# Key blocks of a cross-attention kernel: one PSUM read by ScalarE, and the low halves made from SBUF by GpSimd and VectorE

## The reference

```
x = layernorm(x + self_attention(x))
kv = ctx @ wkv.T + bkv;  k, v = split(kv)          # ctx: (16, 1500, 256)
q = qdq(x) @ qdq(wq).T + bq                        # int8-like rounding
p = softmax(q k^T / sqrt(16));  o = p v            # 16 heads
x = layernorm(x + qdq(o) @ qdq(wp).T + bp)
x = layernorm(x + experts(x))                      # top 2 of 8
```

## Time and profile before

| | |
|---|---|
| median of 3 runs | 853.0 us (848.32 to 858.43) |
| the profiled execution | 854.35 us, its span 852.5 us |
| mean granted TensorE clock | 0.986 |
| PE busy | 774.4 us, 91% of the span |
| DVE busy | 638.2 us, 75% |
| ACT busy | 511.5 us, 60% |
| POOL busy | 296.9 us, 35% |
| the chain that ended last | PE 57%, DVE 13%, DMA 11%, ACT 10%, issue 6% |

### The profile page before, as it was taken

How to read it: one execution, slowest core, us unless ns; L and a number is a source line. 1 busy time by engine, 2 the same in 40 slices (tenths; PEclk the granted TensorE clock), 3 DMA queues, 4 the chain that set the end, 5 groups by cost and what they waited for, 6 DMA issues and landing times.

```text
span 852.5 us, 30042 instructions
## 1 busy us (share of the span) xinstructions
PE 774.4 (91%) x12379; PEld 582.8 (68%) x12379; DVE 638.2 (75%) x1234; ACT 511.5 (60%) x1084; POOL 296.9 (35%) x366
## 2 busy tenths in 40 slices
PE   5689989999998999999999999999898899999996
PEld 3366666576666666666666666666665579999995
DVE  5877777868877878785977778786875745688887
ACT  2347656566565657655665666666665543787772
POOL 3263216223712371254126421732270003143232
PEclk9899999999999999999999999999999899999999
DMA  7356554554645546554655655565467976766643
GB/s 228 91 167 174 169 155 139 156 160 128 179 129 159 164 143 180 164 143 138 178 156 141 173 169 147 154 171 156 121 186 208 307 258 161 225 190 209 210 136 98
DMA packets 91380, 143.27 MB, mean 168 GB/s; under 512 B 11423, under 2 KB 79583, under 8 KB 87918
## 3 DMA queue, kind: packets, MB, share of 16 engines
q1 hardware_dynamic: 87742, 136.74, 53.6%
q0 software_dynamic: 3504, 4.62, 2.8%
HBM read 101.60 MB, written 39.68 MB: 166 GB/s over the span
## 4 chain that ended last, share of the span: by engine, by line
PE 57%; DVE 13%; DMA 11%; ACT 10%; issue 6%; SPq 1%; POOL 1%; DVEq 0%; POOLq 0%; ACTq 0%
PE ps L1659 15%; PE ps L1652 11%; DMA sums<-y_sb,g_token 10%; PE ps L1733 7%; PE ps L1711 6%; DVE negmax L522 4%; ACT pT L1441 3%; ACT k_front L1414 3%; PE ps L1971 3%; PE ps L1675 3%; DVE k_front L516 2%; PE ps L1992 2%; PE ps L1776 2%; PE ps L1620 2%; PE ps L1743 2%
## 5 line engine op out<-in xcount | busy, mean ns | idle before, releaser
L522 DVE TENSOR_REDUCE negmax<-ps 112x1 f32<-112x1500 f32 x121 | 207.4, 1714 | 32.1 <-PE ps L1675 31.9
L1441 ACT ACTIVATE pT<-ps 125x448 f32<-125x448 f32 x384 | 195.7, 546 | 21.9 <-PE ps L1711 18.2
L1265 POOL TENSOR_TENSOR ctx_lo<-ctx_raw,ctx_hi 128x250 f16<-128x250 f32 x188 | 119.3, 666 | 182.4 <-DVE ctx_hi L507 182.4
L1711 PE MATMUL ps<-qbd,k_st 97*128 97x112 f16 x1536 | 127.8, 214 | 17.3 <-ACT pT L1441 8.7
L1711 PEld LDWEIGHTS ps<-qbd,k_st 97*128 97x128 f16 x1536 | 91.2, 98 | 73.6 <-ACT pT L1441 20.1
L1397 ACT COPY v_sb<-ps 125x512 f32<-125x512 f32 x96 | 56.4, 587 | 83.5 <-PE ps L1659 83.4
L516 DVE SCALAR_TENSOR_TENSOR k_front<-ps,bk_sb,k_front 128x500 f16<-128x500 f32 x80 | 58.8, 735 | 63.0 <-ACT k_front L1414 63.0
L1733 PE MATMUL ps<-pT,v_sb 125*17 125x56 f32 x6144 | 92.1, 215 | 12.2 <-issue 12.2
L1733 PEld LDWEIGHTS ps<-pT,v_sb 125*17 125x17 f32 x6144 | 79.9, 98 | 31.9 <-issue 20.1
L1414 ACT ACTIVATE k_front<-ps,bk_sb 128x500 f16<-128x500 f32 x80 | 54.3, 678 | 62.3 <-PE ps L1652 62.3
L1659 PE MATMUL ps<-wkv_hi,ctx_hi 128*125 128x256 f16 x384 | 76.6, 281 | 10.5 <-DVE k_front L516 9.0
(11 more groups left out here) (263 smaller groups left out, 1492.7 us busy)
## 6 DMA issues: line engine op xcount, KB each, us to landing
k_st<-k_dram SPq DMA_DIRECT2D x288, 125.0 KB, 3.0
w_sb<-w SPq DMA_DIRECT2D x25, 1024.0 KB, 5.2
ctx_raw<-ctx_T SPq DMA_DIRECT2D x48, 500.0 KB, 3.7
k_dram<-k_front SPq DMA_DIRECT2D x80, 250.0 KB, 3.0
xs<-zeros SPq DMA_DIRECT2D x28, 260.0 KB, 4.4
w_sb<-w SPq DMA_DIRECT2D x8, 512.0 KB, 5.2
k_dram<-k_back SPq DMA_DIRECT2D x16, 250.0 KB, 2.9
xg<-xs SPq DMA_DIRECT2D x21, 130.0 KB, 4.1
```

The lines of the kernel that those rows point to most:

```text
L522: V.tensor_reduce(negmax[0:QW], ps[0:QW, BANK_S:BANK_S + CHUNKS, 0:MC], AX.XY, ALU.max, negate=True).then_inc(max_done, 1)
L1265: last = nc.gpsimd.tensor_tensor(ctx_lo[:, k, c2, a], ctx_raw[:, k, c2, a], ctx_hi[:, k, c2, a], ALU.subtract)
L1441: nc.scalar.activation(pT[0:MT, (PAIRS * b + p) % 3, TPC * g:TPC * g + TPC], ps[0:MT, BANK_T + n % 2, 0:TPC * QW].rearrange("p (t n) -> p ...
L1711: last = mm(ps[:, BANK_T + n % 2, QW * i:QW * i + QW], k_st[:, j, p, a:a + P], qbd[:, j, p].rearrange("p h s -> p (h s)"), start=True, sto ...
```

## The change

ACT now reads a key block from PSUM once and writes it as f32 to SBUF (`k_full`, a ring of three); this releases the bank (`unit_out`). DVE rounds that copy to the f16 high half (`tensor_copy` into the ring `k_two`, also of three), after a wait for the store of the block three before it. The remainder is a subtraction of two SBUF operands: on GpSimd as two pieces of 250 columns (`k_lo_step`), and on DVE as one piece of 500 columns (`key_low`) for all six blocks of batch 0 and, in slot 3 of each even batch, for units 0 and 2 of the odd batch being prepared. The stores wait for the remainder (`k_lo_done`). `two_batches` is as before.

```
         def unit_step(b, par, u):
             if g in KEYS:
-                i = key_place(c, g)
-                dve.wait_ge(unit_done, UNITS * b + u + 1)
-                dve.wait_ge(k_hi_done, len(KEY_UNITS) * b + KEY_UNITS.index(u) + 1)
-                V.scalar_tensor_tensor(k_two[i][:, 1], ps[:, BANK_KV, 0:MC], bk_sb[:, g:g + 1], k_two[i][:, 0],
-                                       ALU.add, ALU.subtract).then_inc(unit_out, 1)
+                n = key_number(b, u)
+                dve.wait_ge(unit_out, UNITS * b + u + 1)
+                if n >= 3:
+                    dve.wait_ge(*stored(n - 3))
+                V.tensor_copy(k_two[:, n % 3, 0], k_full[n % 3]).then_inc(k_hi_done, 1)
+                if b == 0:
+                    key_low(b, u)
+        def key_low(b, u):
+            n = key_number(b, u)
+            dve.wait_ge(k_hi_done, n + 1)
+            dve.wait_ge(k_lo_done, n)
+            V.tensor_tensor(k_two[:, n % 3, 1], k_full[n % 3], k_two[:, n % 3, 0], ALU.subtract).then_inc(k_lo_done, 1)
...
                     if units_on:
                         for u in unit_slots(slot):
                             unit_step(b + 1, 1 - j, u)
+                    if slot == 3 and j == 0:
+                        key_low(b + 1, 0)
+                        key_low(b + 1, 2)
...
             def store_keys(b, u, between=()):
-                sp.wait_ge(unit_out, UNITS * b + u + 1)
+                sp.wait_ge(k_lo_done, n + 1)
                 if not (isinstance(b, int) and b == 0):
                     sp.wait_ge(k_in[g], loaded(b - 1))
-                sp.dma_start(k_dram[i], k_two[i]).then_inc(stored(b, u)[0], 16)
+                sp.dma_start(k_dram[i], k_two[:, n % 3]).then_inc(stored(n)[0], 16)
...
+            def k_lo_step(b, u):
+                n = key_number(b, u)
+                pool.wait_ge(k_hi_done, n + 1)
+                if b % 2 == 1 and u == 5:
+                    pool.wait_ge(k_lo_done, n)
+                for half in range(2):
+                    a = slice(MC // 2 * half, MC // 2 * half + MC // 2)
+                    last = nc.gpsimd.tensor_tensor(k_two[:, n % 3, 1, a], k_full[n % 3][:, a], k_two[:, n % 3, 0, a], ALU.subtract)
+                last.then_inc(k_lo_done, 1)
             def iteration(it, t_before):
-                ctx_lo_step(2 * it + 1, 1, 1)
+                b = 2 * it + 1
+                ctx_lo_step(b, 1, 1)
...
                 kbd_step(it + 1)
-                ctx_lo_step(2 * it + 1, 1, 2)
-                ctx_lo_step(2 * it + 2, 0, 0)
+                ctx_lo_step(b, 1, 2)
+                k_lo_step(b, 5)
+                k_lo_step(b, 6)
+                k_lo_step(b, 8)
+                ctx_lo_step(b + 1, 0, 0)
                 if t_before is not None:
                     b_rstd_step(t_before)
-                ctx_lo_step(2 * it + 2, 0, 1)
+                k_lo_step(b, 11)
+                ctx_lo_step(b + 1, 0, 1)
+                k_lo_step(b + 1, 0)
+                k_lo_step(b + 1, 2)
                 rstd_step(it + 1)
-                ctx_lo_step(2 * it + 2, 0, 2)
+                ctx_lo_step(b + 1, 0, 2)
+                k_lo_step(b + 1, 5)
+                k_lo_step(b + 1, 6)
+                k_lo_step(b + 1, 8)
                 qbd_step(it + 1, 0, 0)
-                ctx_lo_step(2 * it + 3, 1, 0)
+                ctx_lo_step(b + 2, 1, 0)
                 qbd_step(it + 1, 0, 1)
+                k_lo_step(b + 1, 11)
...
             def k_hi_step(b, u):
                 c, g = UNIT[u]
-                i = key_place(c, g)
-                if b > 0:
-                    act.wait_ge(*stored(b - 1, u))
+                n = key_number(b, u)
                 act.wait_ge(unit_done, UNITS * b + u + 1)
-                nc.scalar.activation(k_two[i][:, 0], ps[:, BANK_KV, 0:MC], ACT.Identity,
-                                     bias=bk_sb[:, g:g + 1]).then_inc(k_hi_done, 1)
+                if n >= 3:
+                    act.wait_ge(k_lo_done, n - 2)
+                nc.scalar.activation(k_full[n % 3], ps[:, BANK_KV, 0:MC], ACT.Identity, bias=bk_sb[:, g:g + 1]).then_inc(unit_out, 1)
```

More of the change, by code:

```diff
@@ L161, in decoder_layer @@
         wkv_lo = sb("wkv_lo", [P, CH, 2 * D], F16)
-        k_front = sb("k_front", [P, 5, 2, MC], F16)
+        k_two = sb("k_two", [P, 3, 2, MC], F16)
+        k_full01 = sb("k_full01", [P, 2, MC])
         sb("behind_k_front", [P, 8], F32)
@@ L168, in decoder_layer @@
         k_st = sb("k_st", [KA, 2, PAIRS, M + 4], F16)
-        k_back = sb("k_back", [P, 2, MC], F16)
+        k_full2 = sb("k_full2", [P, MC])
         sb("behind_keys", [P, 616])
@@ L220, in decoder_layer @@
         b_oqT = a_t2[:, D:D + P].bitcast(BF16).rearrange("p (c n) -> p c n", c=CH)
-        k_two = [k_front[:, n] for n in range(5)] + [k_back]
+        k_full = [k_full01[:, 0], k_full01[:, 1], k_full2]
         staging = pT[:].rearrange("p a m n -> p (a m n)")
@@ L273, in decoder_layer @@
         k_hi_done = sem("k_hi_done")
+        k_lo_done = sem("k_lo_done")
         unit_out = sem("unit_out")
@@ L434, in key_place, with key_number, stored @@
             return CH * c + g
-        def stored(b, u):
-            n = KEY_UNITS.index(u)
-            return k_out[n % 2], 16 * (len(KEY_UNITS) // 2 * b + n // 2 + 1)
+        def key_number(b, u):
+            return len(KEY_UNITS) * b + KEY_UNITS.index(u)
+        def stored(n):
+            return k_out[n % 2], 16 * (n // 2 + 1)
         def loaded(b):
@@ L1082, in store_keys @@
                 c, g = UNIT[u]
-                i = key_place(c, g)
-                sp.wait_ge(unit_out, UNITS * b + u + 1)
+                i, n = key_place(c, g), key_number(b, u)
+                sp.wait_ge(k_lo_done, n + 1)
                 if not (isinstance(b, int) and b == 0):
                     sp.wait_ge(k_in[g], loaded(b - 1))
-                sp.dma_start(k_dram[i], k_two[i]).then_inc(stored(b, u)[0], 16)
+                sp.dma_start(k_dram[i], k_two[:, n % 3]).then_inc(stored(n)[0], 16)
                 for dst, src in between:
@@ L1094, in load_keys @@
                 i = key_place(c, g)
-                sp.wait_ge(*stored(b, u))
+                sp.wait_ge(*stored(key_number(b, u)))
                 for r, part in enumerate(KEY_PARTS[c]):
@@ L1293, in qbd_step @@
                     pool.wait_ge(st_done, CHUNKS * PAIRS * (2 * t + j - 1))
-                if j == 1:
+                if j == 1 and (h == 1 or t == 0):
                     pool.wait_ge(qbd_done, 8 * t + 4 + 2 * h)
+                elif j == 1:
+                    pool.wait_ge(k_lo_done, 2 * len(KEY_UNITS) * t + len(KEY_UNITS))
+                elif h == 0 and not first:
+                    pool.wait_ge(k_lo_done, 2 * len(KEY_UNITS) * t + len(KEY_UNITS) - 1)
                 elif first and h == 0:
@@ L1375, in _ @@
             ctx_lo_step(B - 1, 1, 2)
+            k_lo_step(B - 1, 5)
             b_rstd_step(TILES - 2)
+            for u in (6, 8, 11):
+                k_lo_step(B - 1, u)
             scatter(TILES - 2)
```

## The result

| | before | after |
|---|---|---|
| median of the runs | 853.3 us (4 runs) | 906.3 us (4 runs, 903.3 to 910.3) |
| ratio, 95% interval | | 1.062 (1.055 to 1.070) |
| profiled execution, its span | 854.35, 852.5 us | 903.31, 901.5 us |
| mean granted TensorE clock | 0.986 | 0.953 |

The change makes the kernel 53 us slower. The forecast was 885, slower, with a range from 860 to 908. The sign and the main mechanism were right, the size was short by 21 us.

A forecast was written before the change was run, and what follows sets the result against it. PE was taken to set the pace nearly everywhere. Terms -11 (release, shorter piece), +2 (door), +1 (start), +33 (even batches), +2 (odd), +5 (clock) gave +32: 885 us beside the 853.0 median, range 860 to 908.

The forecast's parts named there:

- The release and the shorter piece: PE's waits on the PSUM bank, 8 us won, and DVE's cast at 0.42 us, 3 us won: 11 us, bounds 3 and 17.
- the door's +2: DVE's 96 casts held by POOL: 16 us of DVE's queue, about one eighth on the chain, 2 us, bounds 0 and 12.
- The two engines at one door: DVE's casts and subtractions from SBUF can be held for one POOL piece; a cast waits 0.17 us on average.
- The stalls in even batches: Slot 4's scores wait for unit 11's loads behind the store moved to slot 3: 33 us in eight batches, bounds 25 and 44.
- its door term: Within the even batches' stall, slot 3's first subtraction held by POOL's `kbd` pieces: 0.3 us, bounds 0 and 1.04.
- The odd batches: Unit 0's remainder on POOL delays the same store and loads; cover 1.6 us in seven batches, 2 us added, bounds 0 and 10.
- The clock: TensorE falls to 1.2 GHz behind 4 of eight stalls: 5 us more, bounds 0 and 14.
- small terms: 1 us at the start, from batch 0's six remainders on DVE, and 2 us for the odd batches.
- A: Rival: unit 11's load isn't late, so only the release counts, 844 us; chance 0.06.
- B: Rival: no change, with shorter stalls of 25 us, the gain at its bound of 17 and the clock holding, 861; chance 0.08.
- C: Rival: DVE becomes the bound, each of 96 casts held for a full POOL piece, odd batches at their bound, 912; chance 0.08.

The follow-up runs named there:

- the kernel with the early subtractions: The changed kernel, with VectorE making the remainders of units 0 and 2 of odd batches right behind their casts in slots 1 and 2: 845.6 us, repeated 845.1 us.
- all remainders on GpSimd: The changed kernel, with GpSimd also making the remainders of units 0 and 2 of odd batches, in slot 2 ahead of `kbd`: 861.9 us, 1.010.
- the late store alone: The kernel before, with the store of unit 0 of each odd batch waiting for `nm_row` of slot 3 of the batch ahead: 905.7 us, 1.059.
- `kbd` behind: The changed kernel, with GpSimd's `kbd_step` waiting until VectorE has made the remainders of units 0 and 2: 895.6 us, 1.048.
- the kernel with the load ahead: The changed kernel, with unit 11's load of the running batch ahead of the store of unit 0 in SP's order: 855.0 us, 1.004.

## Why the prediction was right, and where it was short

**The release and the shorter piece: -11 with the door's +2, so -9.** Measured -10, as 855.3 against 845.1 us in the kernel with the early subtractions, where no store is late; only the sum of these terms was measured. The cast took 0.421 us at the median, where 0.42 stood between 0.16 and 0.68.

**The two engines at one door.** Two effects have to be kept apart. Casts took 0.52 us on average, 0.10 more than undisturbed and 10 us in all, where 16 were expected. But the hold of `key_low` was put at 0.3 us, with a bound of 1.04, one piece of `kbd`. For the first subtraction, on which the store hangs, it was 3.0 to 3.7 us in batches 4 to 12, 0.0 and 0.4 in batches 0 and 2, and none in batch 14: 17 us in eight batches against 2.4. This is the term that failed, together with its bound. It was taken from line 507, a cast, which got in between two pieces at that very place after 0.24 us. The kind of instruction doesn't make the difference: subtractions got in between two pieces in batches 0 and 2 of the changed kernel, and a cast was held for the whole run in the kernel with the early subtractions. What differs is GpSimd's queue. In all traces here DVE was held for the whole run only where `kbd` began within 0.03 us of the end of the scatter, and for at most one piece where GpSimd stood idle for 0.7 us or more before `kbd`, or came to it straight from its own subtractions (all remainders on GpSimd, batches 0 and 2). In the kernel before it stood idle for 1.35 us there; in the changed kernel GpSimd, with the remainders to make, comes to it later, and the idle time is gone. Whether the scatter is the cause, and by what in the hardware, was not tried. The Trainium skill, "SBUF — State Buffer", section "Who interferes with whom", says that the engine that issues first keeps the shared pair for the whole instruction. The trace goes beyond that: DVE was ready at 499.07, during the first of four instructions, and came in after the fourth, at about 502.4.

**The stalls in even batches: +33.** Measured 50.5, beyond the bound of 44. With the hold taken out, some 33 are left, where the forecast without its door term was 31; the late store alone gave 32 in a kernel without the hold, and 38 were left with `kbd` behind. The chain from the row of maxima is otherwise as worked out: in batch 10, 0.34 + 0.04 for the store, the third load 0.98 later, landing within 2.93. In batch 14 the 6.9 us come from elsewhere: SP issues a piece of the expert weights between that store and the loads (1.25 us), and they land later beside it. This was in the code and not counted.

**The odd batches: +2.** Measured nothing. The cover of 1.6 us was enough, and no stall there is over 0.2 us.

**The clock: +5.** Measured 12. Four falls were counted and eight came, and each lasted 6.8 to 10.2 us, where the one in the earlier trace rows lasted 3.4. The bound of 14 held.

**The sum.** 50.5 + 12 - 10 = 52.5 us, against 53.0 measured. It was forecast as 33 + 5 - 9 and 3 for small terms. The stalls passed their bound by 6 us, and the measured time lies only 2 us inside the range: that the range held was partly luck. The odd batches, which cost nothing where up to 10 were allowed, made up for it. The rivals fell: A needed the load to be early, B a short stall, and C a DVE queue that bounds; in the kernel with the load ahead DVE does the same work in 855 us.

## What to carry to other kernels

When a step is moved, follow every queue past the instruction that waits for it: here a store moved by two slots took three loads of another batch with it, and these were worth 50 us where the edit itself was worth 10. A wait for an engine that shares a door can last for the whole run of instructions that the other has queued, and not for one of them; its bound is to be set by the run, even where a row shows one piece. And a stall of 4 to 7 us of TensorE is dearer than its length, here by a quarter, through the clock behind it.

## What the runs showed of the hardware that was not expected

- A subtraction of two SBUF operands on DVE took up to 4.37 us instead of 0.68 while GpSimd had four instructions of 1.0 us queued, and a cast from SBUF up to 4.06. With GpSimd's run moved behind it, the subtraction took at most 1.29 us.
- The same run of GpSimd held DVE for all four instructions where it began 0.02 us behind a scatter, and for one at most where GpSimd had stood idle for 0.7 us or more, or came straight from subtractions. That the scatter is the cause was not shown.
- The clock fell with PE busy 4.00 of 4 us, on matmuls of 32 rows and 112 columns of weights. It did not fall in the same place with matmuls of 128 by 128. So PE's busy time alone doesn't tell these two apart.
- A wait of one store, added to an otherwise unchanged kernel, cost 52 us with 32 us of visible waits.
